# Routed experts of a gated two-layer block on one core: weights stationary and loaded per tile, against activations stationary and experts resident

## The chip, the cores and the metric

One core of one Trainium2 chip. The metric is the device time of one execution in microseconds; for the kernel before it is the median of three runs.

## The reference, cut to what matters

Two parts in a row on x of 4 x 256 tokens of 256 values: graph attention over a context (two layers, 8 heads), then a mixture of experts. The change touches the second alone.

```python
def _L0_ffn_ref(x, w_router, wg, wu, wd, sg, su, sd):
    E, TOPK, H, I, NSH = (8, 2, 256, 640, 2)
    xt = x.reshape(-1, h)                                   # 1024 tokens
    scores = jax.nn.sigmoid(jnp.einsum('th,eh->te', xt, w_router))
    topk_w, topk_i = jax.lax.top_k(scores, TOPK)
    topk_w = topk_w / jnp.sum(topk_w, axis=-1, keepdims=True)
    comb = jnp.zeros((T, E)).at[jnp.arange(T)[:, None], topk_i].add(topk_w)
    gate = jax.nn.silu(jnp.einsum('th,eih->tei', xt, wg))
    up = jnp.einsum('th,eih->tei', xt, wu)
    expert_out = jnp.einsum('tei,ehi->teh', gate * up, wd)
    out = jnp.einsum('te,teh->th', comb, expert_out)
    sgate = jax.nn.silu(jnp.einsum('th,jih->tji', xt, sg))  # two shared experts
    sup = jnp.einsum('th,jih->tji', xt, su)
    return (out + jnp.einsum('tji,jhi->th', sgate * sup, sd)).reshape(b, s, h)

x = x + jnp.tanh(g_xattn[0]) * _L0_xattn_ref(ctx_512, _layernorm(x), ...)
x = x + jnp.tanh(g_ffn[0]) * _L0_ffn_ref(_layernorm(x), ...)
```

## The kernel before, in words

All operands are fp32 but for some scores. The program is written engine by engine, with semaphores by hand; each engine runs its list in the order written.

**Up to the routed stage.** 32 attention units (8 graph layers of 4 units) run through TensorE, ScalarE and VectorE. Fillers between them compute the two shared experts for all 1,024 tokens (`gate_up` at line 592: weights stationary, 256 tokens moving; `down` at 602: hidden values stationary, weights moving). For each of the four batches of 256 tokens the router picks two experts per token (`choose`, `place`), and GpSimd sends each token's normalised row, with its weight and its number, to a place in `slots` in DRAM, sorted by expert (`send_rows`, L400). `save_base` (L1106) writes residual plus shared output to y_sb, and ScalarE's queue stores it to `out` (`store_base`, L880).

**The table.** Each expert's rows are cut into tiles of 128; there are always 23 tiles (SLOT_TILES, 2,048 rows plus padding). `make_table` writes for each tile its row in `slots` (row_i) and its expert (expert_i).

**Weights.** An expert is 3,840 values per partition: 2,560 of gate and up (two k halves), 1,280 of down; 1,920 KB in all. The tensor `weights` holds eight routed and two shared experts. Three routed ones are loaded after the fill of `slots` (L315), five later (L321), because the attention's scratch lies on their place. TensorE waits for all eight before the first routed step (line 801) and finds a tile's expert by a register (`expert_at`, line 754).

**A routed step s** in TensorE's order (`step`, line 779): gate and up of tile s, chunk 0 (256 of the 640 hidden columns; `gate_chunk`, L749: the tile's 128 tokens stationary, 512 columns of gate and up weights moving, two k halves); transposes of the next input tile (L738); transposes of the hidden values of tile s-1, 5 of them (`turn_hidden`, L765); chunks 1 and 2 (256 and 128 hidden columns); down of tile s-1 (L775: hidden values stationary, 256 columns moving, 5 matmuls). ScalarE takes tanh of each chunk (L935), copies the transposed input (L939) and the transposed hidden values (L950). VectorE makes silu times up of each chunk (L1091, L1094) and, first in its step s, scales the output of tile s-2 by the token weights (`scale_output`, L1280).

**Queues.** SP loads the input tiles (`load_tile`, L328) into six buffers; tile j+6 waits for r_add of tile j. GpSimd adds each scaled tile to `out` with an indirect DMA (`add_tile`, L439), and waits for its landing before the next; y_sb has two buffers, and `scale_output` of tile j waits for the add of tile j-2. Tiles 0 to 3 are written out, 18 run in loops of six, the rest is written out again.

Of the kernel before, what the change touches and what calls it, by code (L numbers as in the profile page):

```python
# [14 lines left out]
P = 128  # L15
# [5 lines left out]
HV = N // P  # L21
# [17 lines left out]
W_EXP = KC * GU + IC * D  # L39
# [77 lines left out]
def build(nc, x, ctx_t, w0, w1, params, bias_t, w_router, w_experts, slots, out):  # L117
    with ExitStack() as stack:
# [19 lines left out]
        hid = hidden[:, 0:2 * I].rearrange("p (s i) -> p s i", s=2)  # L138
        hid_t = hidden[:, 2 * I:4 * I].rearrange("p (s i n) -> p s i n", s=2, i=IC)
# [9 lines left out]
        LATE = 5  # L149
        scratch_at = [(E - LATE) * W_EXP]  # L150

        def carve(shape, dt=F32):
            n = 1
            for s in shape[1:]:
                n *= s
            n = n if dt == F32 else (n + 1) // 2
            a = scratch_at[0]
            scratch_at[0] = a + n
            assert scratch_at[0] <= E * W_EXP
# [60 lines left out]
        ld_expert = [sem(f"ld_expert{e}") for e in range(E)]  # L220
# [23 lines left out]
        r_ht, r_htc, r_y, r_ysb = sem("r_ht"), sem("r_htc"), sem("r_y"), sem("r_ysb")  # L244
# [3 lines left out]
        w_exp = weights.rearrange("p (e w) -> p e w", e=E + NSH)  # L248
# [35 lines left out]
        def _(sp):  # L284
# [22 lines left out]
            sp.dma_start(w_exp[:, E:E + NSH, :], w_experts[E:E + NSH].rearrange("e p w -> p e w")).then_inc(ld_shared, 16)  # L307
# [21 lines left out]

            for j in range(SLOTS_IN):  # L330
                load_tile(j, j)
            FULL = SLOT_TILES // SLOTS_IN - 1
            with sp.Fori(1, 1 + FULL) as q:
                for s in range(SLOTS_IN):
                    j = SLOTS_IN * q + s
                    sp.wait_ge(r_add, 16 * (j - SLOTS_IN + 1))
                    load_tile(j, s)
            for j in range(SLOTS_IN * (1 + FULL), SLOT_TILES):
                sp.wait_ge(r_add, 16 * (j - SLOTS_IN + 1))
                load_tile(j, j % SLOTS_IN)  # L340
            sp.wait_ge(r_add, 16 * SLOT_TILES)
# [109 lines left out]
        def _(pe):  # L451
# [140 lines left out]
            def gate_up(n, i, dst):  # L592

                base = (E + i // IC) * W_EXP
# [7 lines left out]
            def down(n, half, e, dst):  # L602
                for i in range(IC):
                    a = (E + e) * W_EXP + KC * GU + i * D
# [148 lines left out]

            def expert_at(q, r):

                e = pe.value_load(expert_i[0:1, bass.ds(SLOTS_IN * q + r, 1)], min_val=0, max_val=E - 1)
                return e * W_EXP

            def turn_hidden(q, r):
                j = SLOTS_IN * q + r  # L760
                pe.wait_ge(r_hid, 3 * j + 3)
                if not isinstance(j, int) or j >= 1:
                    pe.wait_ge(r_htc, j)
                for i in range(IC):
                    mm = pe.transpose(ps_pt[:, i * P:(i + 1) * P], hid[:, r % 2, i * P:(i + 1) * P], ident)  # L765
                mm.then_inc(r_ht, 1)

            def down_tile(q, r):
                j = SLOTS_IN * q + r
                off = expert_at(q, r)  # L770
                pe.wait_ge(r_htc, j + 1)
                if not isinstance(j, int) or j >= 1:
                    pe.wait_ge(r_ysb, j)
                for i in range(IC):
                    mm = pe.matmul(ps_o[:, 0:D], hid_t[:, r % 2, i, :],  # L775
                                   weights[:, bass.ds(off + (KC * GU + i * D), D)], start=(i == 0), stop=(i == IC - 1))
                mm.then_inc(r_y, 1)

            def step(q, r):
                s = SLOTS_IN * q + r  # L780
                inner = not isinstance(s, int)
                off = expert_at(q, r) if inner or s < SLOT_TILES else None
                if off is not None:
                    gate_chunk(q, r, 0, off)
# [4 lines left out]
                if off is not None:  # L789
# [11 lines left out]
            for e in range(E):  # L801
                pe.wait_ge(ld_expert[e], 16)
# [11 lines left out]
        def _(act):  # L814
# [126 lines left out]
            def step(q, r):  # L941
# [6 lines left out]
                if inner or s >= 1:  # L948
                    act.wait_ge(r_ht, s)
# [398 lines left out]
```

## Time and profile before

| | us |
|---|---|
| median of three runs | 445.16 (443.85 to 445.98) |
| profiled execution, its time | 445.5 |
| its span in the profile | 443.7 |
| TensorE matmul busy | 395.6 (89%) |
| TensorE weight load busy | 289.1 (65%) |
| VectorE busy | 257.2 (58%) |
| ScalarE busy | 205.5 (46%) |
| GpSimd busy | 90.5 (20%) |
| moved by DMA | 42.48 MB |

The span is what the profile's rows add up to; the device time of that same execution is 1.8 us longer. PE is TensorE's matmuls, PEld its weight loads, which run beside them; DVE is VectorE, ACT ScalarE, POOL GpSimd, SP the queue that issues most transfers. The page cuts the span in 40 slices of 11.1 us and gives the busy share of each in tenths. Other views group instructions by line, follow the chain of waits that ended last, sum each engine in a window, or list instructions in order of time. A window's columns are its length, the busy time of PE, PEld, DVE, ACT and POOL with their instructions, the granted clock, the DMA share and GB/s. An fp32 matmul shows as two matmul instructions, each with a weight load; a transpose as one.

### The profile page before, as it was taken

Reading aid. Unit: us, or ns where it says so; the run is one execution under the profiler, and the core shown is the slowest. Engines: PE = TensorE matmul, PEld = TensorE weight load, DVE = VectorE, ACT = ScalarE, POOL = GpSimd, SP = SyncE. Lnnn points to the kernel's source line nnn. Section 1 sums busy time; section 2 is a strip of 40 time slices with the busy share of each in tenths; the row PEclk is TensorE's granted clock in tenths of the full one; section 3 lists DMA queues with packets and bytes.
Section 4 is the critical chain, followed back from the end, with each engine's and each line's share of the span. In section 5 each row is a group of like instructions: output and inputs, shape, how many; then the busy total and the mean of one; then the engine's idle time right before and its main releaser. Section 6 shows DMA issues by size and latency. Waiting matters only on the chain.

```text
span 443.7 us, 7225 instructions
## 1 busy us (share of the span) xinstructions
PE 395.6 (89%) x2295; PEld 289.1 (65%) x2296; DVE 257.2 (58%) x814; ACT 205.5 (46%) x519; POOL 90.5 (20%) x100
## 2 busy tenths in 40 slices
PE   3877787787988999997999999999999999999991
PEld 2445464555765878776888886666667676766660
DVE  3799999899887784785474424343333333433330
ACT  4597999999854668420120213232232323232320
POOL 6656140001000022121312000212121212121221
PEclk9998999999998999998999999999999999999997
DMA  6199999100000001000698300122212222221212
GB/s 172 27 353 343 339 354 429 60 1 1 1 1 1 2 7 67 1 24 27 242 429 347 88 2 24 26 36 38 36 38 39 35 46 33 39 36 24 24 12 24
DMA packets 22988, 42.48 MB, mean 96 GB/s; under 512 B 1968, under 2 KB 20976, under 8 KB 21680
## 3 DMA queue, kind: packets, MB, share of 16 engines
q1 hardware_dynamic: 17632, 35.76, 23.3%
q0 software_dynamic: 4080, 5.18, 7.4%
q10 hardware_dynamic: 1248, 1.18, 0.8%
q8 instruction: 16, 0.26, 0.2%
q14 instruction: 12, 0.10, 0.1%
HBM read 24.81 MB, written 17.31 MB: 95 GB/s over the span
## 4 chain that ended last, share of the span: by engine, by line
PE 59%; DVE 19%; ACT 14%; POOL 3%; issue 2%; DMA 2%; POOLq 0%; DVEq 0%
PE ps_z L749 13%; PE ps_o L775 11%; PE ps_gu L749 9%; ACT weights L843 6%; PE ps_pt L605 5%; PE ps_z L598 5%; DVE weights L1041 5%; PE ps_gu L598 4%; DVE weights L1036 3%; ACT weights L834 3%; ACT weights L849 3%; PE ps_pt L765 3%; PE ps_gu L605 2%; DVE hidden L1094 1%; DVE gate_silu L1091 1%
## 5 line engine op out<-in xcount | busy, mean ns | idle before, releaser
L439 POOL DMA_INDIRECT out<-y_sb,tile_in x23 | 35.9, 1559 | 166.1 <-DVE y_sb L1280 163.0
L843 ACT ACTIVATE weights<-weights 128x256 f32<-128x256 f32 x128 | 64.3, 536 | 0.1
L749 PE MATMUL ps_z<-weights,tile_t 128*128 x184 | 63.2, 486 | 0.0
L775 PE MATMUL ps_o<-weights,hidden 128*128 x230 | 53.5, 380 | 0.9 <-ACT hidden L950 0.9
L1091 DVE SCALAR_TENSOR_TENSOR gate_silu<-gate_tanh,ps_z 128x256 f32<-128x256 f32 x66 | 24.5, 371 | 49.5 <-ACT gate_tanh L935 36.2
L517 PE MATMUL ps_pt<-ident,weights 128*128 128x128 f32 x256 | 35.4, 284 | 15.6 <-ACT weights L849 15.2
L749 PEld LDWEIGHTS ps_z<-weights,tile_t 128*128 128x128 f32 x184 | 33.2, 190 | 23.2 <-issue 22.0
L775 PEld LDWEIGHTS ps_o<-weights,hidden 128*128 128x128 f32 x230 | 43.6, 190 | 7.0 <-issue 1.1
L935 ACT ACTIVATE gate_tanh<-ps_gu 128x256 f32<-128x256 f32 x23 | 8.8, 383 | 80.5 <-PE ps_gu L749 80.5
L517 PEld LDWEIGHTS ps_pt<-ident,weights 128*128 128x128 f32 x256 | 29.9, 147 | 22.6 <-issue 21.8
L1036 DVE SCALAR_TENSOR_TENSOR weights<-weights 128x1024 f32<-128x1024 f32 x32 | 39.0, 1219 | 9.1 <-ACT weights L834 5.6
L1091 DVE SCALAR_TENSOR_TENSOR gate_silu<-gate_tanh,ps_gu 128x256 f32<-128x256 f32 x43 | 18.0, 420 | 45.2 <-ACT gate_tanh L935 35.3
L749 PE MATMUL ps_gu<-weights,tile_t 128*128 x92 | 43.2, 592 | 0.0
L598 PE MATMUL ps_gu<-x_norm_t,weights 128*128 128x256 f32 x160 | 39.6, 391 | 4.1 <-DVE hidden L1094 4.1
L834 ACT ACTIVATE weights<-ps_z 128x1024 f32<-128x1024 f32 x32 | 33.5, 1047 | 8.7 <-PE ps_z L508 8.7
L598 PE MATMUL ps_z<-x_norm_t,weights 128*128 128x256 f32 x160 | 37.3, 382 | 0.0
L598 PEld LDWEIGHTS ps_gu<-x_norm_t,weights 128*128 128x128 f32 x160 | 29.7, 192 | 9.1 <-DVE hidden L1094 5.6
L386 POOL TENSOR_TENSOR weights<-weights,minus_half 128x2 f32<-128x2 f32 x8 | 7.5, 940 | 132.3 <-DVE weights L1010 132.3
L849 ACT ACTIVATE weights<-ps_pt 128x1024 f32<-128x1024 f32 x32 | 33.5, 1046 | 0.8 <-PE ps_pt L517 0.8
L598 PEld LDWEIGHTS ps_z<-x_norm_t,weights 128*128 128x128 f32 x160 | 29.8, 190 | 4.1 <-issue 0.4
L935 ACT ACTIVATE gate_tanh<-ps_z 128x256 f32<-128x256 f32 (+1 forms) x46 | 15.2, 330 | 34.7 <-PE ps_z L749 34.7
L505 PE MATMUL ps_z<-weights 96*128 96x512 bf16 x64 | 27.3, 426 | 4.3 <-DVE weights L1026 2.9
(192 smaller groups left out, 618.4 us busy)
## 6 DMA issues: line engine op xcount, KB each, us to landing
weights<-w_experts SPq DMA_DIRECT2D x8, 1920.0 KB, 14.1
slots<-pad_row SPq DMA_DIRECT2D x9, 1188.0 KB, 13.5
weights<-w_experts SPq DMA_DIRECT2D x1, 3840.0 KB, 14.5
tile_in<-slots SPq DMA_DIRECT2D x23, 132.0 KB, 2.1
out<-y_sb ACTq DMA_DIRECT2D x4, 256.0 KB, 2.2
weights<-x SPq DMA_DIRECT2D x2, 256.0 KB, 4.4
x_in<-x SPq DMA_DIRECT2D x2, 256.0 KB, 5.3
out<-y_sb,tile_in POOLq DMA_INDIRECT x23, 3.8
```

The lines of the kernel that those rows point to most:

```text
L439: pool.indirect_dma_start(out=out, out_offset=bass.IndirectOffsetOnAxis(ap=tile_in[:, slot, ID_COL:ID_COL + 1].bitcast(U32), axis=0), in_= ...
L505: pe.matmul(ps_z[:, pair, :], v[0:PART_ROWS, half * P:(half + 1) * P], pick_self[0:PART_ROWS, h:h + 2, :], start=True, stop=False, skip_gr ...
L517: mm = pe.transpose(ps_pt[:, i * P:(i + 1) * P], logits[:, w % AHEAD, i * P:(i + 1) * P], ident)
L598: mm = pe.matmul(dst[:, part * N:(part + 1) * N], weights[:, a:a + P], x_norm_t[n % PAIR][:, k, :], start=(k == 0), stop=(k == KC - 1))
L605: mm = pe.matmul(dst, hid_shared[:, e, i, half * P:(half + 1) * P], weights[:, a:a + D], start=(e == 0 and i == 0), stop=(e == NSH - 1 and ...
L749: mm = pe.matmul(ps_chunk[c][:, 0:2 * cw], tile_t[:, r % 2, k, :], weights[:, bass.ds(off + (k * GU + 2 * c0), 2 * cw)], start=(k == 0), s ...
L775: mm = pe.matmul(ps_o[:, 0:D], hid_t[:, r % 2, i, :], weights[:, bass.ds(off + (KC * GU + i * D), D)], start=(i == 0), stop=(i == IC - 1))
L834: act.activation(logits[:, w % AHEAD, :], ps_z.rearrange("p a n -> p (a n)"), ACT.Copy).then_inc(z_copied, 1)
L843: ins = act.activation(v, v, ACT.Exp, bias=neg_max[:, w % AHEAD, i:i + 1], scale=-1.0, accum_out=sums[:, L % PAIR, s:s + 1])
L849: act.activation(probs_t[:, w % 2, :], ps_pt, ACT.Copy).then_inc(probs_copied, 1)
L1036: dve.scalar_tensor_tensor(out=z, in0=z, scalar=LEAK, in1=z, op0=ALU.mult, op1=ALU.max).then_inc(bent_ready, 1)
L1091: dve.scalar_tensor_tensor(out=gate_silu[:, s, 0:w], in0=gate_tanh[:, s, 0:w], scalar=1.0, in1=gate, op0=ALU.add, op1=ALU.mult).then_inc(r ...
```

## The change

Gate and up of a routed tile are computed with 128 x 128 blocks of weights stationary and the tile's 128 transposed tokens moving, so that the hidden values come out with the hidden index on the partitions, as down needs them; the transposes of hidden values and their copy go. No routed expert is resident: gate, up and down weights of each tile are loaded from DRAM into one of six buffers, behind the tile's own load and in the same queue, in rows of 5 KB (three parts of 1,280 values per partition). The address comes from expert_i in SP's registers. In TensorE's step, down of tile s-1 now stands after the input transposes and ahead of chunks 1 and 2. VectorE scales tile s-1 after chunk 0 of step s, and waits for the four base stores ahead of step 1.

```diff
+W_GU, W_DOWN = KC * GU, IC * D
+W_EXP = W_GU + W_DOWN
+SHARED_AT, RING_AT = 0, NSH * W_EXP
+LD_PARTS = 3
...
+        ring = [weights[:, RING_AT + i * W_EXP:RING_AT + (i + 1) * W_EXP] for i in range(SLOTS_IN)]
...
-        hid = hidden[:, 0:2 * I].rearrange("p (s i) -> p s i", s=2)
-        hid_t = hidden[:, 2 * I:4 * I].rearrange("p (s i n) -> p s i n", s=2, i=IC)
+        hid_t = hidden[:, 0:2 * I].rearrange("p (s i) -> p s i", s=2)
...
-            for e in range(E - LATE):
-                sp.dma_start(w_exp[:, e, :], w_experts[e]).then_inc(ld_expert[e], 16)
...
+            def load_weights(j, place):
+                e = sp.value_load(expert_i[0:1, bass.ds(j, 1)], min_val=0, max_val=E - 1)
+                sp.dma_start(ring[place].rearrange("p (c w) -> p c w", c=LD_PARTS),
+                             w_routed[bass.ds(e * (LD_PARTS * P), LD_PARTS * P), :].rearrange("(c p) w -> p c w", p=P)).then_inc(ld_ring[place], 16)
...
-            for e in range(E - LATE, E):
-                sp.dma_start(w_exp[:, e, :], w_experts[e]).then_inc(ld_expert[e], 16)
...
             for j in range(SLOTS_IN):
                 load_tile(j, j)
+                load_weights(j, j)
             FULL = SLOT_TILES // SLOTS_IN - 1
             with sp.Fori(1, 1 + FULL) as q:
                 for s in range(SLOTS_IN):
                     j = SLOTS_IN * q + s
                     sp.wait_ge(r_add, 16 * (j - SLOTS_IN + 1))
                     load_tile(j, s)
+                    load_weights(j, s)
...
-            def gate_chunk(q, r, c, off):
+            def gate_chunk(q, r, c):
                 j = SLOTS_IN * q + r
                 c0, cw = GATE_CHUNKS[c]
                 if c == 0:
+                    pe.wait_ge(ld_ring[r % SLOTS_IN], 16 * (q + r // SLOTS_IN + 1))
                     pe.wait_ge(r_xtc, j + 1)
                 if not isinstance(j, int) or j >= 1:
                     pe.wait_ge(r_hid, 3 * j + c - 2)
-                for k in range(KC):
-                    mm = pe.matmul(ps_chunk[c][:, 0:2 * cw], tile_t[:, r % 2, k, :],
-                                   weights[:, bass.ds(off + (k * GU + 2 * c0), 2 * cw)],
-                                   start=(k == 0), stop=(k == KC - 1))
+                for i in range(cw // P):
+                    for part, col in enumerate(gate_col(c0 // P + i)):
+                        for k in range(KC):
+                            a = k * GU + col
+                            mm = pe.matmul(ps_chunk[c][:, part * cw + i * P:part * cw + (i + 1) * P], ring[r % SLOTS_IN][:, a:a + P],
+                                           tile_t[:, r % 2, k, :], start=(k == 0), stop=(k == KC - 1))
                 mm.then_inc(r_gu, 1)
...
             def down_tile(q, r):
                 j = SLOTS_IN * q + r
-                off = expert_at(q, r)
-                pe.wait_ge(r_htc, j + 1)
+                pe.wait_ge(r_hid, 3 * j + 3)
                 if not isinstance(j, int) or j >= 1:
                     pe.wait_ge(r_ysb, j)
                 for i in range(IC):
-                    mm = pe.matmul(ps_o[:, 0:D], hid_t[:, r % 2, i, :],
-                                   weights[:, bass.ds(off + (KC * GU + i * D), D)], start=(i == 0), stop=(i == IC - 1))
+                    mm = pe.matmul(ps_o[:, 0:D], hid_t[:, r % 2, i * P:(i + 1) * P],
+                                   ring[r % SLOTS_IN][:, W_GU + i * D:W_GU + (i + 1) * D], start=(i == 0), stop=(i == IC - 1))
...
                 if inner or s + 1 < SLOT_TILES:
                     turn_in(q, r + 1)
                 if inner or s >= 1:
-                    turn_hidden(q, r - 1)
-                if off is not None:
-                    gate_chunk(q, r, 1, off)
-                    gate_chunk(q, r, 2, off)
-                if inner or s >= 1:
                     down_tile(q, r - 1)
+                if inner or s < SLOT_TILES:
+                    gate_chunk(q, r, 1)
+                    gate_chunk(q, r, 2)
...
-                if inner or s >= 1:
-                    act.wait_ge(r_ht, s)
-                    act.activation(hid_t[:, (r - 1) % 2, :, :].rearrange("p a b -> p (a b)"), ps_pt[:, 0:I], ACT.Copy
-                                   ).then_inc(r_htc, 1)
...
-                if inner or s >= 2:
-                    scale_output(q, r - 2)
                 if inner or s < SLOT_TILES:
                     hidden_chunk(q, r, 0)
+                if inner or s >= 1:
+                    scale_output(q, r - 1)
+                if inner or s < SLOT_TILES:
                     hidden_chunk(q, r, 1)
                     hidden_chunk(q, r, 2)
...
-            for s in range(2):
-                step(0, s)
+            step(0, 0)
             dve.wait_ge(st_base, 16 * B)
```

The arrays of weights are laid out on the host, outside the time.

## Rows read from the trace of the kernel before

**Rows 1.** The page: busy times, TensorE's slices, GB/s.

```profile
PE 395.6 (89%) x2295; PEld 289.1 (65%) x2296; DVE 257.2 (58%) x814; ACT 205.5 (46%) x519; POOL 90.5 (20%) x100
PE   3877787787988999997999999999999999999991
GB/s 172 27 353 343 339 354 429 60 1 1 1 1 1 2 7 67 1 24 27 242 429 347 88 2 24 26 36 38 36 38 39 35 46 33 39 36 24 24 12 24
```

**Rows 2.** Chain of waits, last stretch: start us, length us, what.

```profile
421.20 2.16 PE ps_o L775 x10
423.36 1.72 PE ps_gu L749 x4
...
431.67 3.89 DMA out<-y_sb,tile_in
...
436.37 1.55 POOL out L439
```

**Rows 3.** Windows: attention, late expert loads, routed stage.

```profile
163.70:173.70 10.00, 10.00 (x102) 8.37 (x101) 4.88 (x13) 6.79 (x19) 4.72 (x5) 1.00 0.16 56
222.00:234.00 12.00, 12.00 (x62) 10.49 (x61) 9.20 (x43) 2.30 (x6) 2.22 (x3) 1.00 1.02 429
300.00:400.00 100.00, 100.00 (x402) 67.63 (x401) 36.63 (x97) 28.31 (x70) 21.77 (x14) 1.00 0.24 38
```

**Rows 4.** Timeline of one routed step, TensorE matmuls.

```profile
300.43 1.88 PE L749 MATMUL ps_gu<-weights,tile_t 128*128 x4
302.14 0.38 PE L738 MATMUL ps_t<-ident,tile_in 128*128 128x128 f32 x2
302.36 0.71 PE L765 MATMUL ps_pt<-ident,hidden 128*128 128x128 f32 x5
302.90 2.75 PE L749 MATMUL ps_z<-weights,tile_t 128*128 x8
305.49 2.32 PE L775 MATMUL ps_o<-weights,hidden 128*128 x10
```

**Rows 5.** Timeline at the first router, TensorE: matmuls, then weight loads.

```profile
116.26 0.95 PE L578 MATMUL ps_t<-router_w,x_norm_t 128*128 128x8 f32 x8
...
117.04 1.60 PEld L598 LDWEIGHTS ps_gu<-x_norm_t,weights 128*128 128x128 f32 x8
```

**Rows 6.** Timeline: gate's loads after the hidden transposes, and its matmuls.

```profile
288.36 0.30 PEld L749 LDWEIGHTS ps_z<-weights,tile_t 128*128 128x128 f32 x2
...
288.46 2.75 PE L749 MATMUL ps_z<-weights,tile_t 128*128 x8
```

**Rows 7.** Groups by line from 250 on: a full fp32 load's listed length.

```profile
L749 PEld LDWEIGHTS ps_z<-weights,tile_t 128*128 128x128 f32 x184 | 33.2, 190 | 23.2 <-issue 22.0
```

**Rows 8.** Timeline of the end: hidden chain, down, scaling of the last tile.

```profile
428.04 2.32 PE L775 MATMUL ps_o<-weights,hidden 128*128 x10
...
428.90 0.29 DVE L1094 SCALAR_TENSOR_TENSOR hidden<-gate_silu,ps_z 128x128 f32<-128x128 f32 x1
...
431.80 2.42 PE L775 MATMUL ps_o<-weights,hidden 128*128 x10 [0.89 <-ACT hidden L950]
434.26 0.48 DVE L1280 TENSOR_SCALAR y_sb<-ps_o,tile_in 128x256 f32<-128x256 f32 x1 [3.38 <-PE ps_o L775]
```

**Rows 9.** Timeline of SP's queue: issue of the first input tile.

```profile
244.59 0.35 SPq L328 DMA_DIRECT2D tile_in<-slots  x1
```

**Rows 10.** Timeline of TensorE at the start of the routed stage.

```profile
267.02 1.88 PE L749 MATMUL ps_gu<-weights,tile_t 128*128 x4
```

**Rows 11.** The line of the base stores: issues, and issue to landing.

```profile
L880 ACTq DMA_DIRECT2D out<-y_sb x4: 378/378/418, 175.7 to 271.7; - x4
DMA to landing us min/median/max: 2.2/2.2/15.4
```

**Rows 12.** DMA queues, 285 to 430: packets, MB, share of 16 engines.

```profile
q0 software_dynamic: 2880, 2.62, 16.2%
q1 hardware_dynamic: 2448, 2.30, 5.9%
```

More of the change, by code:

```diff
@@ L114, in gate_col, with build @@
     return 2 * c0 + i * P - c0, 2 * c0 + cw + i * P - c0
-def build(nc, x, ctx_t, w0, w1, params, bias_t, w_router, w_experts, slots, out):
+def build(nc, x, ctx_t, w0, w1, params, bias_t, w_router, w_routed, w_shared, slots, out):
     with ExitStack() as stack:
@@ L219, in build @@
         ld_shared = sem("ld_shared")
-        ld_expert = [sem(f"ld_expert{e}") for e in range(E)]
+        ld_ring = [sem(f"ld_ring{i}") for i in range(SLOTS_IN)]
         const_step, ident_ready = sem("const_step"), sem("ident_ready")
@@ L306, in _ @@
                 load_ctx(n)
-            sp.dma_start(w_exp[:, E:E + NSH, :], w_experts[E:E + NSH].rearrange("e p w -> p e w")).then_inc(ld_shared, 16)
+            sp.dma_start(weights[:, SHARED_AT:RING_AT].rearrange("p (e w) -> p e w", e=NSH),
+                         w_shared.rearrange("e p w -> p e w")).then_inc(ld_shared, 16)
             sp.wait_ge(fill_step, 3)
@@ L340, in _ @@
                 load_tile(j, j % SLOTS_IN)
+                load_weights(j, j % SLOTS_IN)
             sp.wait_ge(r_add, 16 * SLOT_TILES)
@@ L592, in gate_up @@
             def gate_up(n, i, dst):
-                base = (E + i // IC) * W_EXP
+                base = SHARED_AT + i // IC * W_EXP
                 for part, col in enumerate(gate_col(i % IC)):
@@ L781, in step @@
                 inner = not isinstance(s, int)
-                off = expert_at(q, r) if inner or s < SLOT_TILES else None
-                if off is not None:
-                    gate_chunk(q, r, 0, off)
+                if inner or s < SLOT_TILES:
+                    gate_chunk(q, r, 0)
                 if inner or s + 1 < SLOT_TILES:
@@ L800, in _ @@
             shared_down(3, 1, 1)
-            for e in range(E):
-                pe.wait_ge(ld_expert[e], 16)
             step(0, 0)
@@ L1285, in step @@
                 inner = not isinstance(s, int)
-                if inner or s >= 2:
-                    scale_output(q, r - 2)
                 if inner or s < SLOT_TILES:
                     hidden_chunk(q, r, 0)
+                if inner or s >= 1:
+                    scale_output(q, r - 1)
+                if inner or s < SLOT_TILES:
                     hidden_chunk(q, r, 1)
                     hidden_chunk(q, r, 2)
-            for s in range(2):
-                step(0, s)
+            step(0, 0)
             dve.wait_ge(st_base, 16 * B)
-            for s in range(2, PEELED):
+            for s in range(1, PEELED):
                 step(0, s)
@@ L1300, in _ @@
                     step(q, r)
-            for s in range(PEELED + SLOTS_IN * ROUTED_LOOPS, SLOT_TILES + 2):
+            for s in range(PEELED + SLOTS_IN * ROUTED_LOOPS, SLOT_TILES + 1):
                 step(0, s)
@@ L1311, with gate_up_rows @@
     from concourse.bass_utils import run_bass_kernel_spmd
-    def expert_rows(gate, up, down):
+    def gate_up_rows(gate, up):
         n = gate.shape[0]
@@ L1321, in expert_rows, with down_rows, all_rows @@
             cols += [g[..., c0:c0 + cw], u[..., c0:c0 + cw]]
-        gu = np.concatenate(cols, -1).transpose(0, 2, 1, 3).reshape(n, P, KC * GU)
-        d = np.asarray(down).transpose(0, 2, 1).reshape(n, IC, P, D).transpose(0, 2, 1, 3).reshape(n, P, IC * D)
-        return np.concatenate([gu, d], -1)
+        return np.concatenate(cols, -1)
+    def down_rows(down):
+        n = down.shape[0]
+        return np.asarray(down).transpose(0, 2, 1).reshape(n, IC, P, D).transpose(0, 2, 1, 3).reshape(n, P, W_DOWN)
+    def all_rows(gate, up, down):
+        n = gate.shape[0]
+        return np.concatenate([gate_up_rows(gate, up).transpose(0, 2, 1, 3).reshape(n, P, W_GU), down_rows(down)], -1)
     arrays = {
@@ L1335 @@
         "w_router": np.asarray(L0_ffn_w_router).transpose(1, 0),
-        "w_experts": np.concatenate([expert_rows(L0_ffn_wg, L0_ffn_wu, L0_ffn_wd),
-                                     expert_rows(L0_ffn_sg, L0_ffn_su, L0_ffn_sd)], 0),
+        "w_routed": all_rows(L0_ffn_wg, L0_ffn_wu, L0_ffn_wd).reshape(E, P, LD_PARTS, W_EXP // LD_PARTS).transpose(
+            0, 2, 1, 3).reshape(E * LD_PARTS * P, W_EXP // LD_PARTS),
+        "w_shared": all_rows(L0_ffn_sg, L0_ffn_su, L0_ffn_sd),
     }
```

32 lines of the change are left out of this document (9 added, 23 removed).

## The prediction

> **What bounds the kernel now.** I read the page first. TensorE is busy for 89% of the span, and at nine tenths in almost every slice from 22 on, [rows 1]; its granted clock is 1.00, the 2.4 GHz level [rows 3]. The chain of waits then says what sets the end: in its last stretch it is TensorE's own work, one group behind another, until the last tile, and then one y, one accumulating store that has to land, and another [rows 2]. The windows confirm it for the routed stage: in the 100 us from 300 on, TensorE is busy for 100 us, VectorE for 37, ScalarE for 28, and the DMA engines have a share of 0.24 [rows 3]. So a routed step costs what TensorE's instructions cost, and nothing else does until something takes over 7.2 us per tile.
>
> One step in the timeline [rows 4]: the 256-column chunk of gate and up starts at 300.43, the input transposes at 302.14, the hidden transposes at 302.36, the two other chunks at 302.90, down at 305.49, and the next step at 307.65 (2.16 later, as in [rows 2]). That is 1.72 + 0.21 + 0.55 + 2.58 + 2.16 = 7.22 us. Every fp32 matmul is two instructions here: 12 of gate and up in 4.30 us (8 of 512 columns at 0.430, 4 of 256 at 0.215), 10 of down at 0.216, and a transpose is one instruction at 0.109.
>
> **Gate and up.** After the change the weights are the stationary side and 128 tokens move. Columns streamed are the same (20 matmuls of 128 against 6 of 512 or 256), but weight loads rise from 12 to 40 per tile. The moving part of a pair costs 0.109 (a transpose streams 128 fp32 columns in that, [rows 4]: 0.55 for 5). The load part: in the router 8 full fp32 loads, each followed by a matmul of only 8 columns, so that nothing but the load counts, run from the first matmul at 116.26 to the next stage's load at 117.04: 0.78 / 7 = 0.112 [rows 5]. Do the two lie beside each other? A gate load that is issued with the last transpose starts at about 288.36 and its matmul runs at 288.46 [rows 6], 0.11 later, while a 128-column instruction is running. So I take 0.112 for a pair, bounds 0.109 (below it the columns bind) and 0.190 (the listed length of a load, [rows 7], if loads did not follow one another closely; the router shows that they do, so the low end is the near one). 40 x 0.1116 = 4.46 us: plus 0.16 per tile. Each ns on the pair is 40 x 23 = 920 ns on the kernel.
>
> The Trainium skill speaks against this. "TensorE: Matmul & The Clock Gate", section "Back-to-back issue gap", says that a stream of weight load and matmul pairs of 128 columns runs at about 81 ns where the matmul alone would take 56, so that loads are not wholly hidden. By an estimate from that page the pair would be some 25 ns longer, 0.137, the gate part 5.5 us and the kernel slower by 14 us. Its numbers are for one-pass matmuls, and the router row disagrees with a surcharge on the load alone; no row has both at 128 columns. It is a rival below.
>
> **Hidden transposes and their copy.** The 5 transposes (0.55 us) leave TensorE, which is the bound: minus 0.55 per tile. ScalarE's copy is off the path but for the last tile, where TensorE waits 0.89 for it [rows 8]. Step: 4.46 + 0.21 + 2.16 = 6.83 us, 0.39 less.
>
> **Order in the step.** down of tile s-1 now stands behind chunk 0 and the input transposes of tile s. It needs the last hidden chunk, and its cover is 16 x 0.112 + 0.21 = 2.0 us. Today that chunk is ready 428.90 + 0.29 - 428.04 = 1.15 us after TensorE leaves it (down starts as the last chunk's columns end, [rows 8]); since chunk 1's two operations on VectorE may now stand closer ahead of it, I make it 1.2. Cost nothing; if it took over 2.0, TensorE would wait for hidden. On VectorE the scaling of y moves between chunk 0 and chunk 1; it waits for down, which ends 4.2 us into the step, and chunk 1 comes at 6.0, so nobody behind it is late. The register loads of TensorE go too: they are hidden today behind full queues, so nothing. TensorE issues 104 instructions per step instead of 58, one per 66 ns; 203 in 10 us, 49 ns each, run in the attention stage with TensorE full [rows 3]. Nothing.
>
> **The eight resident loads.** The last five run in slices 19 to 22, up to about 245 [rows 1]; nobody waits for them at 267, so removing them gives no time. The ring's first load is issued behind the first input tile, at 244.59, and TensorE needs it at 267.02 [rows 9, 10]. At 429 GB/s [rows 3] 1.966 MB take 4.58 us, and a lone store needs 2.2 from issue to landing [rows 11]: 6.8 us, some 15 us of cover. SP's queue holds weights j ahead of tile j+1; so tile 1 lands near 252, against 268.7 (267.02 + 1.72). The sixth set is there by 276; it is needed at 301.
>
> **The steady loads.** Load j+6 waits for the add of tile j, about 17 us after the tile's gate starts (its step 6.8, down by 4.2 in the next, scaling and wake 1.3, landing 4 to 6), and is needed 41 us after it. The engines' need per tile: 4.58 for weights, and what tile and add take now, (16.2% + 5.9%) of 145 us for 20 tiles = 1.60 [rows 12]. 6.2 of 6.83 us: tight, not over. Were it over, the slack of some 17 us has to be eaten first: 17 loads from about 281 to 415 may take 7.9 us each.
>
> **The add.** GpSimd sends one add, waits for it, sends the next: 431.67 to 436.37, 4.70 us, of it 3.9 to landing [rows 2]. Loads will now lie beside it. What a load beside does: the store of 256 KB lands in 2.2 us alone and took 15.4 once, which I put down to the five late loads [rows 11]. It has 16 rows on each engine and a completion, 17 turns: 0.78 us per turn, against 0.57 for one 15 KB row (4.58 / 8). An add has 8 rows and a completion, 9 turns, and the new rows are 5 KB: 0.19 each, or 0.26 by the store's ratio. So 3.9 grows by 1.7 to 2.3, the cycle to 6.4 to 7.0. I take 6.4, because the store also queued behind loads that were issued ahead of it: below 6.83, cost nothing. At 7.0, 17 steps pay 0.17: 2.9 us. What is late next is this chain; VectorE's scaling would wait for it, and behind that the hidden chunks.
>
> **Wait for the base stores.** VectorE now waits for the fourth one before tile 1, not tile 2. It is issued at 271.75 and lands by 274 alone, when that chunk's turn comes anyway; with the first six loads still running it could be 278, costing TensorE 0 to 1 us. I take 0.
>
> **Tail.** Today tile 22's chunk 0 starts at 423.36 and the last add at 436.37, 13.0 us [rows 2]. After: 1.79 + 2.16 (down of 21) + 1.79 + 0.89 = 6.6, hidden 1.2, down to scaling 2.46 (431.80 to 434.26, [rows 8]), scaling 0.48 and GpSimd's wake 0.8 (436.37 less 431.67 + 3.89, [rows 2]): 11.5. The add before it has landed by then. Minus 1.5.
>
> **Sum.** Tile 0 starts at 267.02 as before. Step 0 takes 4.68, 21 more steps 6.83: tile 22 saves 21 x 0.39 less step 0's 0.16, 8.0, and the rows leave 0.2 of the old steps unexplained that I keep: 7.8 us, the tail 1.5: 9.3. The profiled execution took 445.5, its span 443.7: 436.2 by it, 435.9 on the median of 445.16. I say 436.
>
> **Rivals.**
> *Pairs do not overlap fully* (ends slower). Place: the 920 pairs. For it: the load's 190 ns against a matmul of 109, and the skill's rule. Against: [rows 5, 6]. It decides from 0.1116 + 9.3 / 920 = 0.122 us per pair on; at 0.137 the time is 436 + 23 = 459. Chance 0.14.
> *The add's cycle is the bound.* For: 6.4 is near 6.83, and nothing shows an accumulating packet beside a load. Against: the count of turns. At 7.0, 439; at 7.4, 446; at 8.2 (0.38 per turn), 459. Chance 0.17, of it 0.08 faster, 0.03 same, 0.06 slower.
> *The supply of weights falls behind.* It needs under 1.966 / (7.9 - 1.6) = 312 GB/s, and the slowest full slices of the page, with 1 KB rows in them, have 339 [rows 1]. At 280, 8.6 us per load: 17 x 0.7 = 12 later, 448. Chance 0.04.
> *Nothing comes of it* (a load or a wait not seen here takes the 0.39 back, so that the step is again 7.2): 444 to 446. Chance 0.07.
>
> **Numbers.** The forecast as worked out, 433.5 to 441, has 0.58. Faster: 0.58 + 0.08 = 0.66. Within 0.5%, which is about what a measurement of this kernel can tell from no change: 0.03 + 0.07 = 0.10. Slower: 0.14 + 0.06 + 0.04 = 0.24. The range 433 to 448 takes in 0.109 per pair below (2.3 less) and the cheaper end of each rival above, and leaves out some 0.18.
>
> **What would show it.** Right: routed steps of 6.8 us in TensorE's timeline, no idle ahead of its groups, gate and up instructions 0.112 apart, add landings of 5 to 6 us, DMA share near 0.9, no L765 and no L950. Wrong: TensorE waiting for ps_gu's reader with VectorE waiting for the landing of an add (second rival); pairs 0.13 apart with TensorE full (first); TensorE idle ahead of chunk 0 until a weights DMA (third).

## The result, and the profile after

The changed kernel takes 452.15 us (median of 4 runs, 452.06 to 452.64) beside 445.44 (443.85 to 445.98) for the kernel before on the same chip: ratio 1.0148, 95% interval 1.0123 to 1.0173. That is 1.5% slower, where 436 was forecast. Runs more than 1.5% above the fastest of their own kernel are left out of the ratios; that touches e12 and e14 alone. The profiled execution took 452.18, its span is 450.3 against 443.7. The page, with line numbers of the changed kernel (its routed gate and up are at L756, down at L766, the accumulating store at L442, the scaling at L1262):

```profile
PE 392.0 (87%) x2824; PEld 330.3 (73%) x2824; DVE 255.6 (57%) x814; ACT 189.4 (42%) x496; POOL 90.5 (20%) x100
PE   4887786787988999979999999999999997897890
GB/s 176 37 366 340 339 265 0 2 0 2 1 1 1 2 25 47 1 48 2 71 37 230 418 409 137 200 227 329 267 237 332 260 321 233 259 300 227 198 25 23
...
DMA 32%; PE 26%; DVE 18%; ACT 14%; issue 5%; POOL 3%; POOLq 0%; DVEq 0%
...
L766 PE MATMUL ps_o<-weights,hidden 128*128 128x256 f32 x230 | 54.5, 384 | 12.1 <-DVE hidden L1076 12.1
...
out<-y_sb,tile_in POOLq DMA_INDIRECT x23, 6.8
```

TensorE's busy time fell by 3.6 us and yet the span grew [rows 1]. The accumulating store of a tile's output, called the add below, now takes 6.8 us to land (median) instead of the 3.9 of [rows 2], DMA holds 32% of the chain that ended last, and TensorE idles 12.1 us ahead of down, waiting for hidden values. A window of the routed stage tells what did not fail; columns as in [rows 3]:

```profile
300.00:400.00 100.00, 93.59 (x699) 88.62 (x698) 34.75 (x96) 17.80 (x54) 20.22 (x13) 1.00 0.86 277
```

The clock is 1.00 as before, and the DMA engines are not full (0.86, 277 GB/s). Where TensorE is not held up, its step is what was forecast. TensorE's timeline:

```profile
278.90 1.95 PE L756 MATMUL ps_gu<-tile_t,weights 128*128 128x128 f32 x16
280.69 0.38 PE L741 MATMUL ps_t<-ident,tile_in 128*128 128x128 f32 x2
280.91 2.33 PE L766 MATMUL ps_o<-weights,hidden 128*128 128x256 f32 x10
283.07 2.84 PE L756 MATMUL ps_z<-tile_t,weights 128*128 128x128 f32 x24
285.75 1.50 PE L756 MATMUL ps_gu<-tile_t,weights 128*128 128x128 f32 x12
```

From 278.90 to 285.75 are 6.85 us, with 16 pairs in 1.79: 0.112 each. So TensorE can do a tile in 6.85; the adds cannot take one away that fast. The chain of waits in the middle of the stage, and the rows of GpSimd and of SyncE's queue (SPq) beside it:

```profile
340.56 6.55 DMA out<-y_sb,tile_in
347.11 0.02 issue
347.14 0.04 POOLq L440
...
347.23 0.52 issue
347.76 0.04 POOLq L445
347.79 0.19 issue
347.98 6.86 DMA out<-y_sb,tile_in
```

```profile
340.56 1.55 POOL L442 DMA_INDIRECT out<-y_sb,tile_in  x1 [5.97 <-DVE y_sb L1262]
347.98 1.56 POOL L442 DMA_INDIRECT out<-y_sb,tile_in  x1 [5.86 <-DVE y_sb L1262]
...
340.51 0.35 SPq L318 DMA_DIRECT2D tile_in<-slots  x1
341.71 0.39 SPq L322 DMA_DIRECT2D weights<-w_routed  x1
347.92 0.34 SPq L318 DMA_DIRECT2D tile_in<-slots  x1
349.11 0.39 SPq L322 DMA_DIRECT2D weights<-w_routed  x1
```

Two readings. First, the cycle is GpSimd's own: an add lands, 0.87 us pass in its sequencer, the next one goes out, 6.55 + 0.87 = 7.42 us later than the one before. The bracket blames VectorE's y, but in VectorE's timeline the y of the add at 347.98 was scaled at 339.72, long before; the chain, which goes from landing to GpSimd's sequencer, is right. Second, the same landing releases SyncE's loads. So a weight load is issued 0.9 to 1.15 us behind each of the 16 adds from 292.91 to 414.70.

The second add starts at 284.56 and, 17 intervals on, the one at 423.36: 8.16 us each, where TensorE would give one each 6.84 to 6.85. VectorE's scaling waits for the add two tiles back, 61.5 us in all (13 waits), and behind the scaling stand the hidden chunks for which TensorE waits. After 423 the loads are over, and the last adds go out 4.6 to 5.6 apart:

```profile
414.70 7.73 DMA out<-y_sb,tile_in
422.43 0.03 issue
422.45 0.50 DVE y_sb L1262
422.95 0.41 issue
423.36 3.81 DMA out<-y_sb,tile_in
...
442.83 1.55 POOL out L442
```

### The profile page after: what moved, and what is told of

It is laid out like the page before. It is cut to its first block, busy times and chain, and to the rows that moved or that the text cites. A ratio compares the mean times of both kernels' runs of the same rounds, so it can differ in the third digit from the quotient of the medians.

```text
span 450.3 us, 7962 instructions
## 1 busy us (share of the span) xinstructions
PE 392.0 (87%) x2824; PEld 330.3 (73%) x2824; DVE 255.6 (57%) x814; ACT 189.4 (42%) x496; POOL 90.5 (20%) x100
## 4 chain that ended last, share of the span: by engine, by line
DMA 32%; PE 26%; DVE 18%; ACT 14%; issue 5%; POOL 3%; POOLq 0%; DVEq 0%
DMA out<-y_sb,tile_in 31%; ACT weights L829 6%; PE ps_pt L608 5%; PE ps_z L601 5%; DVE weights L1023 4%; PE ps_gu L601 4%; DVE weights L1018 3%; ACT weights L820 3%; ACT weights L835 3%; PE ps_gu L608 2%; PE ps_pt L520 1%; DVE hidden L1076 1%; DVE gate_silu L1073 1%; PE ps_z L756 1%; PE ps_gu L756 1%
## 5 line engine op out<-in xcount | busy, mean ns | idle before, releaser
L442 POOL DMA_INDIRECT out<-y_sb,tile_in x23 | 35.9, 1559 | 172.2 <-DVE y_sb L1262 130.7
L756 PEld LDWEIGHTS ps_z<-tile_t,weights 128*128 128x128 f32 x552 | 65.2, 192 | 1.1
L756 PE MATMUL ps_z<-tile_t,weights 128*128 128x128 f32 x552 | 65.3, 275 | 0.0
L766 PE MATMUL ps_o<-weights,hidden 128*128 128x256 f32 x230 | 54.5, 384 | 12.1 <-DVE hidden L1076 12.1
L766 PEld LDWEIGHTS ps_o<-weights,hidden 128*128 128x128 f32 x230 | 41.9, 190 | 19.2 <-DVE hidden L1076 14.4
L1262 DVE TENSOR_SCALAR y_sb<-ps_o,tile_in 128x256 f32<-128x256 f32 x23 | 11.1, 483 | 73.0 <-DMA out<-y_sb,tile_in 61.5
L520 PE MATMUL ps_pt<-ident,weights 128*128 128x128 f32 x256 | 37.0, 292 | 14.6 <-ACT weights L835 14.3
L520 PEld LDWEIGHTS ps_pt<-ident,weights 128*128 128x128 f32 x256 | 31.1, 151 | 21.7 <-issue 20.9
L756 PE MATMUL ps_gu<-tile_t,weights 128*128 128x128 f32 x368 | 44.8, 275 | 0.0
L756 PEld LDWEIGHTS ps_gu<-tile_t,weights 128*128 128x128 f32 x368 | 43.0, 192 | 0.1
```

What stands on the lines that cost most here:

```text
L442: pool.indirect_dma_start(out=out, out_offset=bass.IndirectOffsetOnAxis(ap=tile_in[:, slot, ID_COL:ID_COL + 1].bitcast(U32), axis=0), in_= ...
L520: mm = pe.transpose(ps_pt[:, i * P:(i + 1) * P], logits[:, w % AHEAD, i * P:(i + 1) * P], ident)
L756: mm = pe.matmul(ps_chunk[c][:, part * cw + i * P:part * cw + (i + 1) * P], ring[r % SLOTS_IN][:, a:a + P], tile_t[:, r % 2, k, :], start= ...
L766: mm = pe.matmul(ps_o[:, 0:D], hid_t[:, r % 2, i * P:(i + 1) * P], ring[r % SLOTS_IN][:, W_GU + i * D:W_GU + (i + 1) * D], start=(i == 0), ...
```

## The experiments

Twelve kernels, each an edit of the changed one but for e9, which is an edit of the kernel before. Every ratio is to the kernel before on the same chip (its medians there are 445.1 to 446.5 us). Theory A: the landing of the add beside the loads sets the cycle. Theory B: the supply of weights falls behind. Theory C: something in the new order of the step does it.

**e2, no loads in the steady state.** The loads of tiles 6 to 22 are gone; those tiles use the weights that the six buffers hold.

```diff
                     load_tile(j, s)
-                    load_weights(j, s)
```

> Left out: the weight loads of tiles 6 to 22; those tiles use what the ring holds, so their weights are other experts'. All else as after the change. Theory A (the add's cycle is the bound, because its landing grows from 3.8 to about 7 us beside a weight load): landings are back at 3.8 to 3.9, the cycle at 4.7, TensorE sets the step at 6.83, and the time is 435 to 437. Theory B (the supply of weights itself is too slow, the adds are only late with it): the same time, so this run does not part A from B, it prices both. Theory C (40 pairs of load and matmul cost more than the columns in the long run, or the new order makes a wait): the time stays within 3 us of 452.

Measured: 438.43 us, 1.4 above the range, ratio 0.980 (0.975 to 0.985). Adds land in 3.8 (median), 5.0 at most.

```profile
300.00:400.00 100.00, 100.00 (x766) 96.34 (x765) 38.57 (x103) 19.66 (x60) 23.33 (x15) 1.00 0.24 39
```

TensorE is full again. The loads are the cause, by whichever way; the step itself is not.

**e3, no add.** The accumulating store is left out.

```diff
                 pool.wait_ge(r_ysb, j + 1)
-                pool.sem_inc(pool_passed, 1)
-                pool.indirect_dma_start(
...
-                    in_=y_sb[:, y_slot, :], in_offset=None, compute_op=ALU.add).then_inc(r_add, 16)
-                pool.wait_ge(r_add, 16 * (j + 1))
+                pool.sem_inc(r_add, 16)
```

> Left out: the accumulating store of the routed outputs (the output holds residual and shared part alone); GpSimd only passes the count on. All weight loads stay. Theory A: without adds nothing waits for a landing; TensorE sets the step at 6.83, and as the tail loses its last add as well, the time is 430 to 434. Theory B: the loads still bind; a tile costs at least the 5.6 us of engine time that 384 rows took, plus 0.5 for the input, with a pause between loads, and the step stays over 7.2 us: over 440.

Measured: 430.5 us, ratio 0.966 (0.961 to 0.970).

```profile
300.00:400.00 100.00, 100.00 (x758) 96.13 (x758) 38.72 (x102) 19.12 (x58) 0.00 (x0) 1.00 0.83 293
```

All loads are there at 293 GB/s and TensorE never waits: B falls. It takes both, loads and adds.

**e4, two thirds of each load.** The third part of a steady load (down's weights) is left out: `load_part` is `load_weights` with the first two of the three parts. Those tiles use the down weights of an earlier tile.

```diff
+PART_LOADED = 2
...
-                    load_weights(j, s)
+                    load_part(j, s)
```

> Left out: the last third of each weight load of tiles 6 to 22 (the down part), so those tiles' down weights are those of an earlier tile. Theory A, by dose: the add's cycle falls from about 8.1 us by a third of its growth over 4.7, to 7.0, and 17 steps are 0.2 over TensorE's 6.83: 438 to 442. Theory B, by dose: a load takes two thirds of its engine time, 3.7 us, far below a step: 436. If the time is above 446, neither scales with the bytes.

Measured: 448.53 us, ratio 1.006 (1.003 to 1.008); landing 6.7 against 6.8. The forecast of A (438 to 442), which scaled the harm with the bytes, was 6.5 us too low at its upper end, and B's 436 was further off. The smaller load lands 6.4 us after its issue and still covers the add issued beside it. That the two meet counts for more than how many bytes the load has.

**e9, experts resident, copied.** The kernel before with the new step; ScalarE copies gate and up weights of the tile's expert (2,560 per partition) to one of two fixed places, over the shared experts' dead weights. No weights are loaded in the routed stage.

```diff
+                e = act.value_load(expert_i[0:1, bass.ds(j, 1)], min_val=0, max_val=E - 1)
+                act.activation(gate_buf[r % 2], weights[:, bass.ds(e * W_EXP, KC * GU)], ACT.Copy).then_inc(r_wcp, 1)
```

> Complete computation. The eight experts are resident and loaded as in the kernel before; ScalarE copies each tile's gate and up weights (2,560 per partition) to one of two fixed places, and TensorE uses them as the stationary side in the new order. No load per tile. The copy should take 2.4 to 2.8 us of ScalarE's 5.8 idle us per step and lie between the tanh of chunk 0 and that of chunk 1. Theories A and B: step 6.83, landings 3.9: 435 to 438, faster than both kernels. Theory C: 450 or more.

Measured: 436.84 us, ratio 0.980 (0.975 to 0.985). Adds land in 3.7 to 3.9.

```profile
300.00:400.00 100.00, 100.00 (x759) 96.13 (x758) 38.83 (x103) 53.51 (x74) 22.02 (x15) 1.00 0.25 39
```

A copy takes 2.34 us and lies beside TensorE's work. This kernel is faster than the one before and the changed one.

**e5 and e6, rows of 15 KB and of 2.5 KB.** Same bytes, other packets (1 and 6 parts instead of 3).

```diff
-LD_PARTS = 3
+LD_PARTS = 1
```

> Complete computation. One edit after the change: a weight load is cut into 128 rows of 15 KB (8 per DMA engine) where it was 384 of 5 KB. Same bytes. Theory A1 (an add's packets take turns with the load's rows, one row per packet, and some rows lie ahead of its first packet): the wait per turn triples until the load is through, so a landing takes as long as the load, 7.5 to 9 us at each add; cycle 8.5 to 10, time 455 to 475. Theory A2 (what delays an add is the load's bytes, however they are cut): landing 6.8 as after the change, time 449 to 453. Theory B (supply): longer rows move a little faster, time 452 or below.

> Complete computation. One edit after the change: rows of 2.5 KB (48 per engine and load). Theory A1: a turn costs about 0.1 us, a landing 3.8 + 0.8 ahead + 0.9 in turns = 5.5, cycle 6.3, under TensorE's 6.83: time 436 to 441. Theory A2: landing 6.8, 449 to 453. Theory B: more rows carry more overhead, 452 or above.

Measured: e5 485.22 us (1.088, 1.082 to 1.095), landing 9.1; e6 439.53 (0.985, 0.979 to 0.992), landing 6.0. The sign and order are A's; e5 came out above its range, with TensorE busy for only 80 of the 100 us from 300 on, at a granted clock of 0.91. The landing does not shrink with the row in proportion: a third of the row (15 to 5 KB) takes 2.3 us off, half of it again 0.8. e6 is in its range for the time, with a landing half a us above the 5.5 expected.

**e8, load ahead of the tile's, released by down.**

```diff
-                    sp.wait_ge(r_add, 16 * (j - SLOTS_IN + 1))
-                    load_tile(j, s)
-                    load_weights(j, s)
...
+                sp.wait_ge(r_y, j - SLOTS_IN + 1)
+                load_weights(j, j % SLOTS_IN)
                 sp.wait_ge(r_add, 16 * (j - SLOTS_IN + 1))
                 load_tile(j, j % SLOTS_IN)
```

> Complete computation. The weight load of tile j+6 is released by down of tile j and stands ahead of the input tile's load in SP's queue; before, it was released by the landing of tile j's add, 5 us later. By the timeline its packets would begin about 2.3 us after down ends, those of the same tile's add about 3.2 us after it. Theory A (overlap in time with the add is what counts): the load still lies over the add's packets, so landings stay at 6 to 8 us and the time at 446 to 455. Theory B (supply): an earlier release gives the loads 5 us more head start each: faster than after the change by several us.

Measured: 459.95 us (1.033, 1.027 to 1.039), landing 7.7. It was slower than A's 446 to 455, and than B allows. But the edit does not let down set the moment: SyncE's queue never waited for down, and its 16 waits from 285 to 420 are all for the landing of an add. SyncE takes its list in order, so a weight load that down has released still stands behind the tile load ahead of it, which waits for an add. The weights of a tile come one add earlier, and yet each load is again issued about 1 us behind an add (343.27 and 344.28). Once it was later. GpSimd's and SyncE's rows:

```profile
351.74 1.55 POOL L436 DMA_INDIRECT out<-y_sb,tile_in  x1 [6.91 <-DVE y_sb L1256]
360.27 1.56 POOL L436 DMA_INDIRECT out<-y_sb,tile_in  x1 [6.98 <-DVE y_sb L1256]
365.04 1.55 POOL L436 DMA_INDIRECT out<-y_sb,tile_in  x1 [3.21 <-DVE y_sb L1256]
...
352.74 0.37 SPq L322 DMA_DIRECT2D weights<-w_routed  x1
361.65 0.37 SPq L322 DMA_DIRECT2D weights<-w_routed  x1
```

With the load 1.00 us behind it, the add of 351.74 holds up the next for 8.53 us; with the load 1.38 behind, the add of 360.27 lands in 3.9 and the next one follows after 4.77.

**e11, load between two adds.** As e8 (the cut shows the difference to it), but released when gate and up of the next tile end, some 2 us behind an add.

```diff
-                sp.wait_ge(r_y, j - SLOTS_IN + 1)
+                sp.wait_ge(r_gu, 3 * (j - SLOTS_IN + 2))
```

> Complete computation. Same loads, same rows of 5 KB, but released by the end of chunk 2 of the next tile's gate and up, some 2.7 us after down, so that its packets begin about 5 us after down ends, when the add's packets (3.2 to 4.5) are through, and end about 9.8, before those of the next add at 10.0. Theory A: nearly every add finds the engines free: landings mostly 3.8 to 4.8, step 6.83, time 435 to 440, with all bytes still moved. Theory B: no gain, as the bytes are the same: 449 to 453. If landings stay at 7 us although load and add do not overlap, A is wrong.

Measured: **436.01 us** (434.61 to 436.78), ratio 0.978 (0.972 to 0.984), span 434.7. Landing 4.6, with the DMA engines fuller than before. Windows, then GpSimd's and SyncE's rows:

```profile
300.00:400.00 100.00, 100.00 (x759) 96.13 (x758) 38.81 (x103) 19.12 (x58) 21.77 (x14) 1.00 0.95 317
```

```profile
332.43 1.55 POOL L436 DMA_INDIRECT out<-y_sb,tile_in  x1 [5.28 <-DVE y_sb L1256]
339.28 1.56 POOL L436 DMA_INDIRECT out<-y_sb,tile_in  x1 [5.30 <-DVE y_sb L1256]
...
334.44 0.37 SPq L322 DMA_DIRECT2D weights<-w_routed  x1
```

Same bytes, same rows, same step; the moment differs, and 16 us are gone. e11 also has the weights ahead of the tile's load in the queue, but so has e8, which differs from it in the release alone and took 459.95. Where the time of an add goes is seen by its packets (queue q0; the loads are q1; packets, MB, share of 16 engines). The DMA view of the changed kernel from 342.00 to 344.00 and 344.00 to 347.00, around the add of 340.56:

```profile
q1 hardware_dynamic: 91, 0.24, 61.7%
...
q1 hardware_dynamic: 183, 0.94, 79.3%
q0 software_dynamic: 144, 0.13, 27.2%
```

Of e9, where no other transfer runs in that stretch, from 335.00 to 336.50 (add at 332.89):

```profile
q0 software_dynamic: 144, 0.13, 81.0%
```

Of e11 from 332.43 to 334.50, and from 334.50 to 336.50 (add at 332.43):

```profile
q1 hardware_dynamic: 192, 0.85, 99.5%
...
q1 hardware_dynamic: 170, 0.32, 51.2%
q0 software_dynamic: 144, 0.13, 45.4%
```

Alone, the 144 packets begin 2.1 us after the issue and go by in 1.3. For the add of 340.56 in the changed kernel they begin 3.5 after it and take 2.7: they start 1.4 later and stream 1.4 longer, which makes up the 2.75 between landings of 6.55 and 3.8. That add is one of the quick ones. By the trace's packets, the means of the 17 adds from 284.56 to 414.70 are a first packet at 4.1 and a stream of 2.8: 2.0 us come from the late start and 1.5 from the stream. In e11 the add of 332.43 has its first packet at 2.1 and is through in 1.7. Not every add of e11 goes so well (the longest landed in 6.5), but the median leaves its cycle under the step.

What makes the start late is not that the engines are busy. In e11 the load before fills them (99.5%) until the add's first packet comes, and it comes as if nothing ran. What goes with it is a load issued close to the add. Of the adds in the ten kernels that load in the steady state, 144 have a load issued between 1.34 us before them and 1.22 us behind, and their first packets come 2.8 to 5.7 us after their issue; 26 have it issued 1.36 to 2.12 behind, and their first packets come at 2.1 to 2.3. The two groups do not touch. Within the first group sooner is worse: with 5 KB rows (the changed kernel, e4, e7, e8) a load 1.1 to 1.2 us behind puts the first packet at 3.3 to 3.8, one 0.97 to 1.03 behind at 3.9 to 4.8, one 0.74 to 0.90 behind at 5.0 to 5.5. Beside the add of 340.56 the load's own first packets come at 342.75, 1.04 us after its issue and 2.2 after the add's; the add's own, due at 2.1, come at 3.5. This fits e8 being slower than the changed kernel as well: its loads are issued mostly 1.00 us behind the add where those of the changed kernel before 370 are mostly 1.13 to 1.15 behind, and its mean first packet is at 4.7 where that kernel has 4.1.

**e7, the old step with the ring.** Tokens stationary, hidden transposes, old order; loads as in the changed kernel.

```diff
-                            mm = pe.matmul(ps_chunk[c][:, part * cw + i * P:part * cw + (i + 1) * P], ring[r % SLOTS_IN][:, a:a + P],
-                                           tile_t[:, r % 2, k, :], start=(k == 0), stop=(k == KC - 1))
+                    mm = pe.matmul(ps_chunk[c][:, 0:2 * cw], tile_t[:, r % 2, k, :],
+                                   ring[r % SLOTS_IN][:, k * GU + 2 * c0:k * GU + 2 * c0 + 2 * cw],
+                                   start=(k == 0), stop=(k == KC - 1))
...
```

> Complete computation. One half of the change alone: the ring of weights stays as after the change (same loads, rows of 5 KB, released by the add), but the step is that of the kernel before: activations stationary, hidden values transposed and copied, down last, scaling first. Theory A: the add's cycle of about 8 us sets the step whichever way TensorE computes, 6.83 or 7.22: 449 to 455, as after the change. Theory C (the stationary form or the new order lost the time): 444 to 447, as before the change.

Measured: 455.67 us (1.019, 1.015 to 1.024), landing 6.8, adds 7.35 to 9.4 apart from 296.65 on. The old step loses by the loads as well: C falls. Its window does not show it yet:

```profile
300.00:400.00 100.00, 99.85 (x402) 67.37 (x401) 34.95 (x94) 27.80 (x69) 18.68 (x12) 1.00 0.86 278
```

TensorE is full there and its steps are 7.22 apart (345.13, 352.35, 359.57), while the adds, at 345.28, 352.75 and 360.46, fall behind it. The loss comes at the end: the last add starts at 447.21, against the 436.37 of [rows 2]. Of the changed kernel's two halves the ring costs. What the new step gains under the ring is small, since the adds bind: 3.5 us by the medians, 2 by the ratios of the two chips, whose intervals (1.015 to 1.024 and 1.012 to 1.017) overlap.

**e13, rows of 1 KB** (the changed kernel with `LD_PARTS = 15`), **e12 and e14, e11 with rows of 2.5 and 15 KB** (`LD_PARTS = 6` and `1`).

> Complete computation. As after the change, rows of 1 KB (120 per engine and load), release by the add. From the landings of 9.1, 6.8 and 6.0 us with rows of 15, 5 and 2.5 KB: 6 to 8 turns and a part of 5.2 us that does not depend on the row, 1.4 over the 3.8 of a lone add. With 1 KB rows the landing is then 5.5 to 5.7 and the cycle 6.3 to 6.5: step 6.83, 435 to 438. If the growth were in turns alone, the landing would be 4.3. If so many rows slow the load itself, its landing grows from 8 us and the time stays at 438 or more.

> Complete computation. Loads released between the adds, rows of 2.5 KB: both remedies. Theory A: TensorE's 6.83 is the bound already with either, so nothing is added: 434.5 to 437, not to be told from 436.

> Complete computation. Loads released between the adds as in the run with rows of 5 KB that took 436, but in rows of 15 KB, the cut that took 485 when the add released them. Theory A: what counts is overlap; with little of it long rows do little harm: 436 to 442. If row size counts by itself, over 460.

Measured: e13 442.79 us (0.993, 0.990 to 0.996). e12 scatters from 440.92 to 448.91 in ten runs, median 447.57; the ratio, from the four up to 446.05, is 0.992 (0.988 to 0.996). e14 has 448.72, 462.28, 464.45 and 478.45 in four, and no ratio. Theory A's forecasts missed in all three; what was expected of e14 if row size counted by itself, over 460, is what three of its four runs took. In e13 landing is 5.9 with 1 KB rows, hardly better than with 2.5 KB: there the packets begin 3.4 or more after the issue as well (add at 339.10, DMA view from 342.50 to 344.50, none in the 3.4 us before it), but those of this add are through in under 2:

```profile
q1 hardware_dynamic: 457, 0.46, 72.1%
q0 software_dynamic: 144, 0.13, 40.9%
```

Over all adds under a load, the mean first packet is at 3.9, 3.8, 4.1 and 4.7 us with rows of 1, 2.5, 5 and 15 KB, and the mean stream takes 2.3, 2.5, 2.8 and 4.3. So the late start hardly depends on the row between 1 and 5 KB; the stream does. Also, small rows delay the base stores, for which VectorE waits ahead of tile 1 (6.6 us in e13), and the first add goes out at 282.20 instead of 277.7. e12 has the same trouble (3.9 us, first add at 279.24): the load released by TensorE, at 279.88, is then 0.64 us behind the add instead of the 1.99 of e11. That add is late, the tile load waits for it, and the next weight load stands behind the tile load, as in e8. All of e12's waits in SyncE's queue from 285 to 420 are for landings, and its adds stay 7.5 to 9.3 apart but for one, whose load came 1.37 behind (5.0). e14 shows both regimes in one run, that of 464.45 (the one that was traced; how the run of 448.72 went is not shown). GpSimd's timeline:

```profile
304.69 1.55 POOL L436 DMA_INDIRECT out<-y_sb,tile_in  x1 [5.29 <-DVE y_sb L1256]
311.52 1.56 POOL L436 DMA_INDIRECT out<-y_sb,tile_in  x1 [5.28 <-DVE y_sb L1256]
319.16 1.55 POOL L436 DMA_INDIRECT out<-y_sb,tile_in  x1 [6.08 <-issue]
330.35 1.56 POOL L436 DMA_INDIRECT out<-y_sb,tile_in  x1 [9.63 <-DMA out<-y_sb,tile_in]
340.52 1.55 POOL L436 DMA_INDIRECT out<-y_sb,tile_in  x1 [8.61 <-DVE y_sb L1256]
```

Six adds up to 311.52 are 6.8 to 7.0 apart, in step with TensorE. The last of them lands in 6.5 us, since the 15 KB rows stretch its stream to 4.1; so the next comes late, with a load 1.22 us behind it, and from there they are 8.4 to 11.2 apart. e11's time holds in its four runs, but its place is fragile: one of its adds, at 380.81, also came late, and its load was still 1.54 us behind. e9's is not, as no load meets its adds.

## Why the prediction was wrong

It was wrong in sign and outside its range, through one step; the second rival is what happened, and it had 0.17.

**The add, the step that failed.** "So 3.9 grows by 1.7 to 2.3, the cycle to 6.4 to 7.0. I take 6.4" and "below 6.83, cost nothing". The cycle was 8.16 on average over 17 intervals, of it 0.9 from landing to the next issue. The term counted the turns of the add's packets among the load's (0.19 us each) and nothing else. That part was near: the stream grew by 1.5 us on average, of 1.7 counted. Left out was that the first packet comes 2.0 us later on average (4.1 us after the issue, not 2.1), at rows of 1 KB too; together the landing grew by 3.5 us, to 7.3 on average, and not by 1.7. Left out too was that this is met at every add: the landing releases the next add and SyncE's load together, so they cannot drift apart. Both ends of the bound were below what came, since [rows 11] was read for its time per turn and scaled down. The reason given for the low end, that the store had queued behind loads issued ahead of it, does not hold either: a load issued 1.15 us behind the add of 340.56 had its first packets out before it. e11 beside e8, which differ in the load's release alone, shows that the moment of the load beside the add is what decides.

**Price of that rival.** It gave 459 for 8.2 us per cycle; 452 came. Up to the add of 423.36 the loss is (8.16 - 6.84) x 17 = 22.4 us, and e11's add of the same tile starts at 400.86, 22.5 earlier. Then the loads end and the chain catches up: the last add starts at 442.83 against 427.18, 15.7 later. The catching up, 6.9 us, was not in the price.

**Gate and up: right.** A pair is 0.112 us (16 in 1.79, above). The Trainium skill, "TensorE: Matmul & The Clock Gate", section "Back-to-back issue gap", would have a pair of 128 columns longer than its matmul alone, by the estimate of the prediction 0.137 us; this trace, with 0.112, disagrees for these fp32 blocks. The first rival did not come.

**Hidden transposes, order, resident loads: right.** The step is 6.84 to 6.85 us against 6.83; e2, e3, e9 and e11 show TensorE full with it.

**Steady loads: right.** "Tight, not over": e11 runs with TensorE full at a DMA share of 0.95 and 317 GB/s, and e3 at 0.83. The third rival is out.

**Wait for the base stores: right for the changed kernel.** VectorE waits 2.5 us, TensorE not at all. e13 and e12 show what hangs on it once the first loads hold the stores up longer.

**Tail and sum: right for e11.** Its span is 434.7, 9.0 less than before, against 9.3 forecast, and its median is 436.01. That is the forecast's number from a kernel with another release; the changed kernel itself did not give it. From the last tile's chunk 0 (415.65) to the last add (427.18) are 11.5 us, as worked out. The span after is thus 9.0 gained and 15.6 (450.3 - 434.7) lost: 6.6 more.

What stays open: by what way a load issued close to the add holds back the add's first packet. GpSimd's own instruction takes 1.55 to 1.56 us with and without it, so the hold-up lies behind that. No run here tells what it is, nor what sets the border between 1.22 and 1.36 us.

## What to carry to other kernels

A small transfer whose landing releases the next one has a cycle. A bulk load beside it must leave that cycle below the step, even where the DMA engines have room: price the landing under load by a row that has one, and if there is none, put both signs in the range. Look at what the landing releases: where it starts the load too, the two meet every time, and releasing the load by another event (here the end of the next tile's gate and up, 2.0 us behind the add) was worth 16 us. Then look in the timeline whether the load really moved: in a queue that works in order another wait ahead of it can keep it where it was (e8, 459.95 us). Where a resident copy exists, a copy by an idle engine (2.34 us of ScalarE per tile) gives the same time without depending on a gap.

## What the runs showed of the hardware

With loads in 15, 5, 2.5 and 1 KB rows released by the landing, the same add (144 packets, 0.13 MB) lands in 9.1, 6.8, 6.0 and 5.9 us (medians), alone in 3.8: shorter rows help, and below 2.5 KB hardly more. Cutting a third of the load's bytes changed the landing by 0.1 us (e4). An add's first packet comes at 2.1 to 2.3 us when the load is issued 1.36 us or more behind it, even with the engines full of an earlier load, and at 2.8 to 5.7 when it is issued up to 1.22 us behind. In e14 the chain of adds has two regimes, one in step with TensorE's 6.8 us and one 8.4 us or more apart, and a single late add moved it from one to the other.
